# A ternary feed-forward layer: the integers' transpose, copy and output product moved one tile later than their rounding

## The reference

```python
def activation_quant(x):
    scale = 127.0 / jnp.clip(jnp.max(jnp.abs(x), axis=-1, keepdims=True), 1e-05, None)
    y = jnp.clip(jnp.round(x * scale), -128, 127) / scale
    ...
def weight_quant(w):
    scale = jnp.clip(jnp.mean(jnp.abs(w), axis=-1, keepdims=True), 1e-05, None)
    quant = jnp.clip(jnp.round(w / scale), -1, 1) * scale
    ...
def bitlinear(x, w):
    x_q = activation_quant(x)
    w_q, scale = weight_quant(w)
    out = jnp.einsum('bsd,hd->bsh', x_q, w_q)
    return out * scale
h = bitlinear(x, w1)          # 256 -> 1024
h = new_gelu(h)
return bitlinear(h, w2)       # 1024 -> 256
# around it:
x = x + jnp.tanh(g_ffn[3]) * _L3_ffn_ref(_layernorm(x, axis=-1), L3_ffn_w1, L3_ffn_w2)
```

## Time and profile before

| | before |
|---|---|
| median of 3 runs | 2503.26 us (2500.88 to 2507.92) |
| the profiled execution, its own time | 2503.51 us |
| its span, first to last instruction | 2501.8 us |
| this stage: its first to its last instruction | about 2398.2 to 2501.8 us of the span |
| TensorE busy over the whole span | 2062.5 us (82%) |
| VectorE busy | 1789.2 us (72%) |
| ScalarE busy | 1514.2 us (61%) |
| GpSimd busy | 930.3 us (37%) |
| mean granted TensorE clock | 0.789 of full speed |

### The profile page before, as it was taken

The page is one execution under the profiler, slowest core; times in us unless marked ns, Lnnn a source line. Parts: engine busy times, 40 slices in busy tenths (PEclk is TensorE's granted clock), DMA queues, the critical chain, the costliest instruction groups (busy, mean ns, idle before and its releaser), DMA issues. The chain is left out here.

```text
span 2501.8 us, 50609 instructions
## 1 busy us (share of the span) xinstructions
PE 2062.5 (82%) x17617; PEld 1136.3 (45%) x17617; DVE 1789.2 (72%) x3578; ACT 1514.2 (61%) x2762; POOL 930.3 (37%) x860
## 2 busy tenths in 40 slices
PE   4867999999987868999967688888888888568856
PEld 1344656565654644788634233333333332434433
DVE  5776755555555578433569899999999999566875
ACT  3454633333346755433325899999999999444565
POOL 5740000000003616000534577777777776224301
PEclk9778999999988979999978555555555555687989
DMA  6352211222223044122220354545455554110101
GB/s 200 83 218 71 69 64 67 67 67 67 67 84 98 3 175 158 40 69 65 80 89 1 64 93 90 93 89 93 91 92 93 90 93 90 17 68 2 29 1 34
DMA packets 384880, 195.41 MB, mean 78 GB/s; under 512 B 312301, under 2 KB 355311, under 8 KB 382703
## 3 DMA queue, kind: packets, MB, share of 16 engines
q1 hardware_dynamic: 381617, 184.47, 29.8%
q0 software_dynamic: 3072, 8.39, 1.0%
HBM read 94.99 MB, written 23.09 MB: 47 GB/s over the span
## 5 line engine op out<-in xcount | busy, mean ns | idle before, releaser
L2509 ACT ACTIVATE qa_e<-qa_S,qa_nb,qa_sq 128x512 uint8<-128x512 f32 (+1 forms) x805 | 708.8, 891 | 15.7 <-DVE qa_nb L2524 8.8
L2520 DVE TENSOR_REDUCE qa_mx<-qa_S 128x1 f32<-128x512 f32 x1024 | 636.9, 682 | 10.1 <-PE qa_S L2475 7.9
L2475 PE MATMUL qa_S<-qa_kT,qa_qb 128*128 128x512 f16 x1024 | 533.2, 608 | 117.0 <-ACT qa_e L2509 104.0
L2451 POOL CAST qa_pT<-qa_eT 128x2048 bf16<-128x2048 uint8 x256 | 483.5, 1891 | 209.8 <-DMA qa_eT<-qa_e 153.8
L2475 PEld LDWEIGHTS qa_S<-qa_kT,qa_qb 128*128 128x128 f16 x1024 | 89.6, 106 | 456.9 <-ACT qa_e L2509 440.9
L1116 POOL MEMSET rms_nothing<- 128x512 f16 x1 | 0.5, 524 | 579.8 <-POOLq L3508 579.8
L913 ACT ACTIVATE moe_ap<-moe_a 128x512 f16<-128x512 f32 x132 | 83.1, 630 | 194.4 <-DVE moe_a L935 194.4
L973 PE MATMUL moe_G<-hT,moe_W 128*128 (+1 forms) x792 | 193.8, 381 | 7.1 <-DVE moe_zero L941 7.1
L982 PE MATMUL moe_O<-moe_W,moe_ap 128*128 (+1 forms) x1584 | 194.5, 273 | 4.1 <-DVE moe_ap L937 4.1
L2484 PEld LDWEIGHTS qa_O<-qa_V,qa_pT 128*128 128x128 bf16 x4096 | 161.8, 107 | 74.1 <-issue 65.7
L973 PE MATMUL moe_U<-hT,moe_W 128*128 (+1 forms) x792 | 192.7, 380 | 0.0
(11 more groups left out here) (441 smaller groups left out, 3453.1 us busy)
## 6 DMA issues: line engine op xcount, KB each, us to landing
moe_wb<-weights_T SPq DMA_DIRECT2D x264, 128.0 KB, 2.8
moe_W<-in_moe_w SPq DMA_DIRECT2D x40, 384.0 KB, 11.7
moe_W<-in_moe_w SPq DMA_DIRECT2D x11, 1152.0 KB, 16.8
moe_xs_rows<-rms_nothing SPq DMA_DIRECT2D x46, 128.0 KB, 1.9
moe_ys_rows<-moe_ys SPq DMA_DIRECT2D x23, 256.0 KB, 2.1
conv_rows<-conv_parts SPq DMA_DIRECT2D x16, 256.0 KB, 3.0
qa_eT<-qa_e SPq DMA_TRANSPOSE x256, 3.0
conv_qst<-conv_rows SPq DMA_DIRECT2D x96, 32.0 KB
```

Of the source, the lines that this page charges most:

```text
L2451: nc.gpsimd.tensor_copy(pT[:, u % RING, :, :].rearrange("p (b r) q -> p b r q", r=2), pairs).then_inc(s_cast, 1)
L2475: nc.tensor.matmul(S[:, bank(m), :], qb[:, g // 2, j, g % 2, :], kT[:, g, q * QW:(q + 1) * QW], start=True, stop=True).then_inc(s_S, 1)
L2509: nc.scalar.activation(e8[:, u % RING, q * QW:(q + n) * QW], S[:, b:b + n, :].rearrange("p b c -> p (b c)"), ACT.Exp, bias=nb[:, u % 2:u % ...
L2520: nc.vector.reduce_max(mx[:, i, q:q + 1], S[:, bank(m + q), :], axis=AXX).then_inc(s_mx, 1)
```

## The change

Each iteration t of the loops used to take tile t through the second rounding, the transpose, the copy and the output product. Now the last three of these are done for tile t - 1 in iteration t:

- TensorE: `down(t - 1)` is the first thing of iteration t, ahead of `turned(t)` and `hidden(t + 2)`; `integers_turned` comes right after `hidden(t + 2)`.
- ScalarE: the copy `turned(t - 1)` stands between `gelu(t + 1)` and `integers(t)`; it used to be `turned(t)`, behind `integers(t)` and `normalise(t + 10)`.
- VectorE: `output(t - 2)` in place of `output(t - 1)`.
- After each loop the calls that are left over follow. No instruction is added or removed, and no buffer is changed.

```diff
@@ tensor
                 for t in range(NB):
+                    if t:
+                        down(t - 1)
                     turned(t)
                     if t + 2 < NB:
                         hidden(t + 2)
-                    down(t)
                     if t % Q == 1 and 1 < (t + 3) // Q < NQ:
                         integers_turned((t + 3) // Q)
+                down(NB - 1)
@@ scalar
                     if t + 1 < NB:
                         gelu(t + 1)
+                    if t:
+                        turned(t - 1)
                     integers(t)
                     if t + 10 < NB:
                         normalise(t + 10)
-                    turned(t)
+                turned(NB - 1)
@@ vector
                 for t in range(NB):
                     rounded(t)
-                    if t:
-                        output(t - 1)
+                    if t >= 2:
+                        output(t - 2)
                     if t >= 2 and t + 6 < NB:
                         if t % Q == 2:
                             steps((t + 6) // Q)
                         integers(t + 6)
+                output(NB - 2)
                 output(NB - 1)
```

## The result

The changed kernel takes 2529.09 us (median of 4 runs, 2526.67 to 2534.98), the kernel before 2502.07 us (median of 4). The ratio is 1.011, with a 95% interval of 1.0092 to 1.0128. That is slower, as forecast, but 27.0 us slower and not 10.8, and outside the range.

What follows compares the result with a forecast made beforehand. The stage was taken as bound by a loop through several engines (GELU, gi, TP, H), not by one. Copy +12.9, TI -1.7 and VectorE -0.4 summed to +10.8 us, giving a median of 2514.0 us, range 2507 to 2521.

Steps and rivals of the forecast that it cites:

- The loop, and the copy in it: ScalarE: the copy moves into the GELU, gi, TP, H loop and delays gi by 0.92 us, 14 times, +12.9 us.
- O hidden by gi: TensorE: O, now ahead of TP, ends before gi is there, with 0.18 us to spare, so costs nothing.
- TI, -0.87 twice: TensorE, tiles 5 and 9: O no longer stands ahead of TI, saving 0.87 us at each place, -1.7 us.
- VectorE, -0.4: VectorE: its work with `steps` fits the 5.51 us tile, so 0.37 us lost up to tile 5 goes, -0.4 us.
- I count one such fall of two, as before: TensorE's clock: one fall behind the two 3.03 us TI gaps; none or two moves the sum by 1.7 us.
- Rival 2: TensorE's clock falls in the usual tile too, up to 1.68 us each, total 2519 to 2534 us; chance 0.08.
- Rivals 3 and 4: 3: copy cheaper than forecast, total within 0.3%, chance 0.09; 4: VectorE's wait for O the true brake, 2496 us, chance 0.04.

Runs made afterwards that it cites:

- e8: The kernel before, with matmuls that feed nothing added in TensorE's idle gaps, five a tile and twelve at the two TI places; ratio 0.9988 to the kernel before.
- e1: The changed kernel with eight matmuls that feed nothing added behind H in each tile; 2511.58 us, ratio 1.0040 to the kernel before.
- e5: The changed kernel with H (and TI) first in TensorE's iteration, ahead of O and TP; 2502.24 us, ratio 0.9924 to the kernel before.
- e3: The kernel before, with only the transposes into TI moved ahead of the output product of their iteration; ratio 1.0000 to the kernel before.
- e4: The changed kernel with the copy behind gi and TensorE taking TP, H, TI, O; 2498.87 us, ratio 0.9983 to the kernel before.
- e12: The changed kernel with VectorE's old order, output(t - 1) behind rounded(t); 2530.36 us, ratio 1.0115 to the kernel before.
- e2: The changed kernel with four matmuls that feed nothing added behind H in each tile; ratio 1.0051 to the kernel before.
- e7: The changed kernel with two matmuls that feed nothing added behind H in each tile; ratio 1.0049 to the kernel before.
- e10: The changed kernel with 30 transposes of 128 columns added behind H in ten of its tiles; 2521.46 us, ratio 1.0081 to the kernel before.
- e11: The changed kernel with four matmuls added ahead of H in the loop, the idle gap in front of O left alone; ratio 1.0128 to the kernel before.

## Why the prediction was wrong

Point by point, by its own steps:

- **The loop, and the copy in it: right.** Without falls the stage takes 96.65 us (e8) in the order of before and 107.61 us (e1) in the new one: 10.96 us more, against a sum of 10.8; 0.28 of the 10.96 lie ahead of GELU 2, where the sum had nothing. The copy takes 0.90 to 0.92 us, a quick tile 5.50 us (forecast 5.51), a TI tile 6.87 (about 6.9), the tail 8.72 instead of 7.80 us. e5 shows the cause from the other side.
- **O hidden by gi: right at the full clock only.** In e1 O starts 2452.75 and TP follows at 2453.78, as O ends and as gi does. In a slow tile O lasts up to 1.89 us and TP comes later than 0.1 us after gi, the sign that the prediction named for O not being hidden.
- **TI, -0.87 twice: right**, in e3 and e4 to 0.01 us.
- **VectorE, -0.4: right.** In e1 the three tiles from GELU 2 take 5.50, 5.51 and 5.50 us. The longer tile does most of it: e4 has the lag in a tile of 4.59 us and still takes 4.95 us once; e12 has the longer tile without the lag, and VectorE makes one tile late, 5.97 us.
- **"I count one such fall of two, as before", with no fall behind the usual gap: wrong.** This is the failed step. For the two TI places the count itself came true, one fall behind two gaps of 3.03 us. What failed is the usual gap of 2.12 us, to which the sum gave no fall: it has eight in eleven tiles. So there are nine slow tiles, and the tail is slowed too. Against the same order without falls (e1) they cost 123.48 - 107.61 = 15.9 us. With before's own fall, 1.7 us, taken off, the stage's 25.15 us are 10.96 + 15.87 - 1.68.
- **Rival 2 was what happened**, and it had a chance of 0.08. Its price, up to 1.68 us each, was near: 13.4 us for nine in the tiles, 1.5 each, and 2.7 us more in the tail. The sign named for it, an H of 3.4 us or more, never came: the longest H is 3.28 us, because the low clock lies over O, TP and H together and not over H alone. What let me put it aside were two rows: the clock had stayed up behind an idle time of 1.4 us in every usual tile, and once even behind 3.15 us. From this I took it that 2.1 us was more likely harmless, being two thirds of a gap that did harm half the time. But such a gap comes in eleven of the thirteen tiles, and none of the rows it rested on has a gap between 1.4 and 3.15 us. The Trainium skill, "TensorE: Matmul & The Clock Gate", in its section on psum-queue depth-cycling, says of another kernel that its short idles between groups of matmuls were frequent enough to make the clock swing between its levels. The changed profile agrees that this happens: its rows of 2 us read 1.00, 0.68, 0.50 and 0.97.
- Rivals 3 and 4 are out. VectorE's waits went, and the tiles did not gain from it.

That the falls come from the longer gap being left empty is shown by e1, e2, e7 and e10, which only put work into it, and by e8 for the one fall of before. How much of it is the length of the gap and how much the work around it stays open (e11 and e3's tail speak against the length alone). Why eight usual gaps of eleven are followed by a fall and three are not, and why one slow tile moved in the next execution, was not tested.

## What to carry to other kernels

Find the loop through the engines first, and ask of a moved instruction whether its new place lies in it; here one copy, moved from a gap into the loop, cost its queue time 14 times. Then ask what the longer loop does to the engine that waits: TensorE's clock is part of the loop's price, and a longer pause that recurs in every tile can cost more than the delay itself (here 15.9 us beside 11.0). When an engine waits for work that its next group doesn't need, move that group ahead: H before the transposes gained 17 to 24 us.

## What was not expected of the hardware

- Adding work made the stage quicker: eight matmuls a tile that feed nothing took the stage from 123.48 to 107.61 us, because the clock stayed at 1.00.
- Between 2.12 us of idle time in each tile (nine slow tiles) and 1.7 us (two, both at the longer gaps of the TI places) lies nearly the whole effect. But gaps of 1.37 and 1.12 us were once followed by a fall, in e3's tail, and with more work ahead of H the gap of 2.12 us had three falls instead of eight (e11).
- 30 transposes in the gap held the clock up as the matmuls did, in all ten gaps filled with them.
- A shorter gap did not mean fewer falls: with TI first (e3) both gaps of 2.28 us were followed by one, with an H of 2.7 to 2.8 us, and in the kernel before one of the two gaps of 3.15 us.
